# Perceiver block: the even parts of the second half's inverse transform, from VectorE to ScalarE and GpSimd

## The reference

```python
x = x + xattn(layernorm(x), ctx, ctx, mask, ...)   # cross attention, 16 heads
x = x + mix(layernorm(x), Wq, bq, Wk, bk, Wv, bv)  # token mixing by circular convolution
x = x + ffn(layernorm(x), W1, W2, Wg, bg)          # 8 experts, top 1, gelu
```

```python
q, k, v = x @ Wq + bq, x @ Wk + bk, x @ Wv + bv
s = sum over tokens of irfft(rfft(k) * rfft(v))
out = irfft(rfft(s) * conj(rfft(q)))               # per token, width 512
```

## Time and profile before

| | us |
|---|---|
| median of 3 runs | 802.04 (801.05 to 802.4) |
| span of the profiled execution, first to last instruction | 799.9 |
| TensorE matmuls busy | 774.2 (97%) |
| VectorE busy | 624.1 (78%) |
| ScalarE busy | 470.1 (59%) |
| GpSimd busy | 239.5 (30%) |
| mean granted TensorE clock, as a share of full speed | 0.989 |

### The profile page before, as it was taken

One profiled execution on the slowest core, in us unless ns is written; L12 is line 12 of the kernel. 1 busy time (PEld: TensorE's weight loads), 2 busy tenths in 40 slices (PEclk: granted clock), 3 DMA queues, 4 the chain that ended last, 5 costly groups with the idle time before them and its releaser, 6 DMA issues.

```text
span 799.9 us, 22201 instructions
## 1 busy us (share of the span) xinstructions
PE 774.2 (97%) x8860; PEld 458.9 (57%) x8860; DVE 624.1 (78%) x990; ACT 470.1 (59%) x847; POOL 239.5 (30%) x413
## 2 busy tenths in 40 slices
PE   9999999999999999999999999996999999999995
PEld 3444545555445555455557544655867866876783
DVE  5977888879787887787768568787887879788870
ACT  4546676656765656665648034246668768866960
POOL 0245334433354333344331200004153232232131
PEclk9999999999999999999999999997999999999998
DMA  8324453344323444233433511102999998998500
GB/s 303 147 64 110 115 150 94 81 108 109 81 56 82 107 108 121 60 87 109 123 56 57 211 53 53 53 0 88 333 366 412 410 354 318 362 343 331 216 32 15
DMA packets 94901, 125.56 MB, mean 157 GB/s; under 512 B 76352, under 2 KB 79168, under 8 KB 83956
## 3 DMA queue, kind: packets, MB, share of 16 engines
q1 hardware_dynamic: 92260, 117.65, 46.0%
q0 software_dynamic: 2576, 7.02, 2.4%
HBM read 100.47 MB, written 6.88 MB: 134 GB/s over the span
## 4 chain that ended last, share of the span: by engine, by line
PE 79%; DVE 11%; ACT 3%; DMA 2%; issue 1%; SPq 1%; POOL 1%; POOLq 0%; DVEq 0%; ACTq 0%
PE bank L1472 58%; PE bank L1867 11%; PE bank L1641 4%; DVE arena L933 3%; PE bank L1839 3%; PE bank L1607 2%; ACT arena L695 2%; DVE arena L989 2%; DVE arena L995 1%; DMA arena<-arena 1%; ACT arena L662 1%; DMA arena<-in_wv_t 1%; PE bank L1826 1%; DVE arena L948 1%; DVE arena L965 1%
## 5 line engine op out<-in xcount | busy, mean ns | idle before, releaser
L1472 PE MATMUL bank<-arena 128*128 128x160 f16 (+9 forms) x3880 | 554.4, 303 | 7.9 <-DVE arena L933 3.6
L1472 PEld LDWEIGHTS bank<-arena 128*128 128x128 f16 (+3 forms) x3880 | 316.1, 99 | 234.5 <-issue 11.3
L662 ACT ACTIVATE arena<-arena 128x256 f16<-128x256 f32 (+5 forms) x302 | 254.1, 889 | 27.2 <-PE bank L1839 10.3
L933 DVE SCALAR_TENSOR_TENSOR arena<-arena 128x2048 f16<-128x2048 f32 (+4 forms) x102 | 200.6, 1988 | 32.0 <-ACT arena L662 31.7
L662 ACT ACTIVATE arena<-bank 128x512 f16<-128x512 f32 x175 | 100.0, 584 | 143.7 <-PE bank L1472 110.3
L933 DVE SCALAR_TENSOR_TENSOR arena<-bank,arena 128x512 f16<-128x512 f32 x174 | 116.8, 682 | 43.9 <-ACT arena L662 40.3
L1867 PE MATMUL bank<-arena 128*128 128x512 f16 x384 | 86.6, 380 | 0.0
L695 ACT ACTIVATE arena<-arena 128x257 f32<-128x257 f32 x128 | 63.5, 498 | 23.1 <-DVE arena L997 23.1
L528 POOL TENSOR_TENSOR arena<-arena 32x1024 f16<-32x1024 f32 (+1 forms) x16 | 34.1, 2134 | 141.2 <-PE bank L1641 139.3
L1867 PEld LDWEIGHTS bank<-arena 128*128 128x128 f16 x384 | 36.2, 98 | 41.1
L545 POOL COPY arena<-arena 32x256 f16 (+1 forms) x128 | 50.3, 393 | 24.0 <-DVE arena L933 11.8
(11 more groups left out here) (116 smaller groups left out, 497.1 us busy)
## 6 DMA issues: line engine op xcount, KB each, us to landing
arena<-in_w SPq DMA_DIRECT2D x64, 1024.0 KB, 7.8
arena<-in_ctx_t SPq DMA_DIRECT2D x15, 1024.0 KB, 5.3
arena<-in_awt SPq DMA_DIRECT2D x3, 1024.0 KB, 7.3
l_dram<-arena SPq DMA_DIRECT2D x4, 512.0 KB, 3.8
x_dram<-arena SPq DMA_DIRECT2D x1, 2048.0 KB, 14.5
arena<-in_wk_t SPq DMA_DIRECT2D x4, 256.0 KB, 4.7
arena<-in_ctx_t SPq DMA_DIRECT2D x4, 256.0 KB, 6.5
arena<-in_wv_t SPq DMA_DIRECT2D x1, 1024.0 KB, 8.3
```

Of the source, the lines that this page charges most:

```text
L662: return a.activation(dst, src, ACT.Copy, scale=scale)
L933: return v.scalar_tensor_tensor(dst, src, scale, h, ALU.mult, ALU.subtract)
L1472: last = m.matmul(out_ap, w, x, start=(n == 0), stop=(n == len(pairs) - 1))
```

## The change

ScalarE copies the even part of each tile of the second half out of PSUM into an SBUF buffer (`even_f`, in the space of the first half's spectrum of v), and GpSimd adds it to the tokens. VectorE keeps the odd part of these tiles and waits for GpSimd's add. The even part of tiles 0 to 3 stays as it was. TensorE's odd transform of a tile waits until its even part has been copied, since they share a bank. On GpSimd the wait for the last unbinding goes; the four adds stand in its place, and the low parts of tiles 2 and 3 move behind the power of group 5.

```diff
--- before.py
+++ after.py
@@ -241,6 +241,7 @@
         spec = [[fa.take([KC, D], F32) for _ in range(2)] for _ in range(3)]
         after_spec = fa.at
         prod = view(dft_off, [2, D], F32)
+        even_f = spec[2][0].rearrange("p k (h n) -> p k h n", h=2)[:, :, 0, :]
 
 
         PW = KC * 512
@@ -292,7 +293,7 @@
         x_biased proj_ps proj_hi proj_free split_hi split_lo s_ps s_free s_max s_neg exp_done
         sums_sc recip_done p_hi p_lo q_ready vl_ready pe_waits pv_ps pv_hi pv_free att_copied
         wo_ps x1_done fold_ps fold_hi fold_free wt_sums wt_halves wt_rows ab_split abias_ps abias_done wt_hi wt_lo spec_ps spec_done
-        products unbound irfft_ps x2_done chain_dve chain_pool pool_waits
+        products unbound even_ps even_out even_added irfft_ps x2_done chain_dve chain_pool pool_waits
         gate_landed l2_shift l2_normal x2_stored l2_stored x_rows_landed own_done xt_ps ids_ps wg_split l2_hi l2_lo lt_ps lt_done logits_ps onehot_done rank_ps count_ps routed
         e_landed0 e_landed1 e_landed2 e_landed3 e_landed4 e_landed5 e_landed6 e_landed7 e_hi e_lo perm_done first_ps xs_done h_ps gelu_done h_hi h_lo
         y_ps y_main y_head y_out ids_done rows_landed scattered ranks_moved""".split()
@@ -589,10 +590,16 @@
 
             for n in range(2, 5):
                 power(n)
-            pool.wait_ge(s["unbound"], 4)
-            for t in LN_GROUPS[4]:
-                l2_lo(t)
+            for t in range(HT, NT):
+                pool.wait_ge(s["even_out"], t - HT + 1)
+                both = x_tok[:, t, :].rearrange("p (h n) -> p h n", h=2)
+                g.tensor_tensor(both, both, even_f[:, t - HT].unsqueeze(1).broadcast_to((P, 2, NF)), ALU.add
+                                ).then_inc(s["even_added"], 1)
+            l2_lo(0)
+            l2_lo(1)
             power(5)
+            l2_lo(2)
+            l2_lo(3)
             l2_lo(LN_GROUPS[5][0])
             l2_lo(LN_GROUPS[5][1])
             power(6)
@@ -868,6 +875,9 @@
                     for t in range(HT):
                         l2_split(t)
             act.wait_ge(s["unbound"], 2)
+            for t in range(HT, NT):
+                act.wait_ge(s["even_ps"], t - HT + 1)
+                a.activation(even_f[:, t - HT], (BA, BB, BE, BF)[t % 4][:, 0:NF], ACT.Copy).then_inc(s["even_out"], 1)
             for t in range(HT):
                 gate_transpose_out(t)
             act.wait_ge(s["l2_shift"], 1)
@@ -1280,9 +1290,12 @@
                 even, odd = bank[:, 0:NF], bank[:, NF:D]
                 both = x_tok[:, t, :].rearrange("p (h n) -> p h n", h=2)
                 dve.wait_ge(s["irfft_ps"], t + 1)
-                v.tensor_tensor(both, both, even.unsqueeze(1).broadcast_to((P, 2, NF)), ALU.add
-                                ).then_inc(s["chain_dve"], 1)
-                dve.wait_ge(s["chain_dve"], next(chain))
+                if t < HT:
+                    v.tensor_tensor(both, both, even.unsqueeze(1).broadcast_to((P, 2, NF)), ALU.add
+                                    ).then_inc(s["chain_dve"], 1)
+                    dve.wait_ge(s["chain_dve"], next(chain))
+                else:
+                    dve.wait_ge(s["even_added"], t - HT + 1)
                 v.tensor_tensor(both[:, 0], both[:, 0], odd, ALU.add)
                 v.tensor_tensor(both[:, 1], both[:, 1], odd, ALU.subtract).then_inc(s["x2_done"], 1)
                 dve.wait_ge(s["x2_done"], t + 1)
@@ -1753,8 +1766,9 @@
                 last.then_inc(s["irfft_ps"], 1)
             spectra(range(16, 24))
             for t in range(HT, NT):
-                back(t, 0)
+                back(t, 0).then_inc(s["even_ps"], 1)
             for t in range(HT, NT):
+                pe.wait_ge(s["even_out"], t - HT + 1)
                 back(t, 1).then_inc(s["irfft_ps"], 1)
             for t in range(HT):
                 gate_transpose(t)
```

## The result

| | before | after |
|---|---|---|
| median, us | 801.63 (801.05 to 802.4, 4 runs) | 808.15 (807.94 to 808.35, 4 runs) |
| span of the profiled execution | 799.9 | 805.9 |
| TensorE busy, us | 774.2 | 775.7 |
| VectorE busy, us | 624.1 | 626.5 |
| ScalarE busy, us | 470.1 | 472.2 |

A forecast was written before the change was run, and what follows sets the result against it. TensorE bounds nearly everywhere, except 545 to 560 us, where engines wait in turn and any delay reaches the end. 3.8 + 1.3 + 0.6 = 5.7 us on 799.9 gives 805.6; plus 2.1 to the median, 807.7 us, range 804.2 to 810.2.

The forecast's parts named there:

- The collisions: At unbind(1, 1), GpSimd's four adds and VectorE's instructions take turns: about 0.96 us each, unbinding 3.8 us later.
- A block over the whole add: At unbind(1, 1), the skill's rule read strictly: each collision costs the whole 1.15 us, four 4.6 instead of 3.8.
- ScalarE's copies: Four even-part copies out of PSUM before the odd transforms, 0.39 us each, hidden under ScalarE's idle 8.19 us: no cost.
- The clock: TensorE's clock may fall in the gap before the odd transforms, costing 1.2 us or nothing; half taken, 0.6.
- GpSimd's order: Two first-half low parts behind the first power delay ScalarE's normalisation and the second power: 1.3 us later.
- The sum: Collisions 3.8, GpSimd's queue 1.3 and clock 0.6: 5.7 us on the profiled span of 799.9.
- VectorE's saved 2.9 us: Four even adds leaving VectorE save at most 2.9 us; the saving turns into waiting before the second power, gain nil at best.
- The shift (L1335): Between the powers, VectorE's shift (0.16) collides with a low part, up to 1.1 us, on the side with slack.
- Collisions that don't matter: Rival: GpSimd's adds leave unbind(1, 1) alone, only the queue term stands, 803.3, no loss measured; chance 0.07.
- VectorE mostly first: Rival: one or two collisions at unbind(1, 1) instead of four, 804.3 to 805.3; chance 0.12.
- The clock back late in the expert work: Rival: half clock lasts 3.6 us longer into the dense expert work, TensorE loses 1.8, 809.5; chance 0.14.
- A gain: Rival: kernel faster, needing the second power before 552.86, so ScalarE's normalisation before 548.68; chance 0.03.

The follow-up runs named there:

- e6: Kernel before the change plus four GpSimd float32 adds on unused data, started as the even transforms of tiles 4 to 7 finish; ratio to the kernel before 1.006.
- e7: Kernel before the change plus four GpSimd memsets, which only write SBUF, started as the even transforms of tiles 4 to 7 finish; ratio to the kernel before 1.0005.
- e4: Changed kernel plus 16 useless matmuls on TensorE between the even and odd transforms; ratio to the kernel before 1.0068.
- e3: Changed kernel with the low parts of tiles 2 and 3 back ahead of the power of group 5; ratio to the kernel before 1.008.
- e5: Changed kernel plus 16 useless matmuls before the odd transforms, and low parts of tiles 2 and 3 back ahead of group 5's power; ratio 1.0058, repeated 1.0066.
- e10: Kernel before the change with VectorE making even adds earlier: tiles 4 and 5 right after unbind(1, 1), tile 6 in the wait for the first power; ratio 1.0001.
- e1: Changed kernel with GpSimd's wait for the last unbinding put back ahead of the four adds; ratio to the kernel before 1.0044.
- e2: Kernel before the change with only the low parts of tiles 2 and 3 moved behind the power of group 5; ratio 1.0047.
- e8: Kernel before the change with VectorE's early even adds and ScalarE's normalisation of tiles 4 and 5 after one of four transposed-tile copies; ratio 1.001.
- e9: Kernel before the change with only ScalarE's normalisation of tiles 4 and 5 moved ahead, after one of four transposed-tile copies; ratio 1.0014.

## Why the prediction was right, and where its sizes were off

- **The collisions** were the right step, in kind and in number. The first add asks at 537.47, which is 538.07 on before's clock (the whole stretch is 0.6 early), four collisions. The size was 3.8 and is 4.28, 1.07 each for 0.96, because an undisturbed float32 add takes 0.11 longer than the low part that stood for it. A block over the whole add would be 4 x 1.24 = 5.0; the rows keep a little overlap, as they did at 67 us. e6 and e7 are what shows the mechanism; the timeline alone only suggests it.
- **ScalarE's copies**: taken at 0.39, hidden. They took 0.38, and TensorE didn't wait for them.
- **The clock** was the mis-sized term: 0.6 taken, as half of a bound of 1.2, and 1.15 measured at power 2 (the change against e4). I had rightly asked whether it falls in the gap (it does, at 542.1), and the working for that case was right: VectorE's own steps cover part of the longer transforms, and the rest reaches the first power, 13.96 for 12.81. Taking half of it was wrong. What I hadn't seen is a second branch, from the end of all four odd transforms through the transposes to ScalarE's four copies, on which the whole 2.2 us arrive. In the changed kernel it ends 0.39 before the other; in e3 it is the one that counts.
- **GpSimd's order**: 1.3 taken, 1.43 measured with the clock kept up (e4 against e5), and by the way that I had worked out: the changed kernel's chain runs through the two late low parts. From the end of the unbinding to ScalarE's normalisation the prediction has 9.39 (550.05 - 540.66), and e4 shows 9.41 (17.39 - 7.98). Yet undoing the order gives nothing back (e3), because of that second branch.
- **The sum** is 5.7, and 6.65 measured at power 2. On the changed kernel's chain the three terms lie one behind the other, each worked out from where the one before ends, so adding them was right: 4.07 at power 2 for 3.8, 1.43 for 1.3, 1.15 for 0.6. The forecast time is nearer (807.7 for 808.15) than the sum, and that is luck: it started from 802.04, the median of three runs, and with a fourth the kernel before is at 801.63.
- **VectorE's saved 2.9 us** are worth nothing, as said: at power 2 it had been ready for 3.5 us (555.4 to 558.90). e10, which takes three of the four even adds out of the chain without GpSimd, measures 1.0001, but its odd transforms also start 0.63 later. The shift (L1335) collided with a low part, 1.11 us, at no cost, as said.
- **The rivals.** Collisions that don't matter: refuted by e6 and e7. VectorE mostly first: the race was won by 0.09 us, and four it was. The clock back late in the expert work: no, its second stretch is 13.6 us in both kernels. A gain: no.

## What to carry to other kernels

Before work is moved to an idle GpSimd, look at what VectorE runs at that moment: beside VectorE instructions with two SBUF inputs, a GpSimd instruction that reads SBUF costs VectorE nearly its whole length each time (1.07 of 1.24 us here), and the kernel as well if the chain runs through VectorE there. Beside instructions with an input in PSUM nothing was stretched (L588 beside L1283 and L1286), but waiting until then may cost the work behind it in the queue (e1: the first power 0.97 later). Follow each delay to the engine step on which the next wait ends. Delays on one chain add up; where two branches end at the same step, the later one counts, and undoing a delay on it gives back only the distance to the other (e3). A wait that grows on TensorE is not paid for when it ends: the matmuls behind it may run at half the clock (5.89 us for 3.69 here).

## What the runs showed that I had not expected

- A step's price depends on what is already late: GpSimd's order costs 3.01 us alone (e2), 1.43 behind the collisions (e5 to e4), and beside collisions and half clock, undoing it could give back 0.39 at most and gave nothing (e3).
- A gap of 4.97 us on TensorE was followed by 4.4 us of float32 matmuls at half clock (544.47 to 548.9), at a cost of 2.2 us (5.89 for 3.69), and the clock was up again by 548.9 while they were still running. The later half-clock stretch didn't change its length for it. In e1, e2, e4, e8 and e9 it was 17.1 us in place of 13.6, for a reason that these runs don't settle.
- 16 useless matmuls in a gap (e4) bring back 1.15 us at power 2, though TensorE's own wait of 1.53 behind them remains. Of this, 0.17 is left at the first expert's matmuls.
